# Filling the unused rows of each expert's region during the last batch's attention

## The reference

```python
x = x + tanh(g_xattn) * (self_attention(ln(x)) + cross_attention(ln(x), ctx)) @ Wp + bp   # 16 heads of 16, 1601 context tokens
xf = ln(x).reshape(8192, 256)
scores = softmax(xf @ Wg)                       # 32 experts
weights, indices = top_k(scores, 4)
for e in range(32):
    pos = nonzero(pair_expert == e, size=4096)  # the tokens that chose e
    out = swiglu(xf[tok], W1[e], W2[e], W3[e]) * w[:, None]
    y = y.at[tok].add(out)
x = x + tanh(g_ffn) * (y + swiglu(xf, Ws1, Ws2, Ws3))
```

## Time and profile before

| | us |
|---|---|
| median of 3 runs | 4883.7 (4883.4 to 4888.8) |
| profiled execution | 4891.1 |
| its span | 4888.3 |
| PE busy | 4346.4 (89%) |
| DVE busy | 3532.4 (72%) |
| ACT busy | 2694.8 (55%) |
| POOL busy | 1646.7 (34%) |

### The profile page before, as it was taken

One profiled execution on the slowest core, in us unless ns is written; L12 is line 12 of the kernel. 1 busy time (PEld: TensorE's weight loads), 2 busy tenths in 40 slices (PEclk: granted clock), 3 DMA queues, 4 the chain that ended last, 5 costly groups with the idle time before them and its releaser, 6 DMA issues. The chain is left out here.

```text
span 4888.3 us, 75159 instructions
## 1 busy us (share of the span) xinstructions
PE 4346.4 (89%) x25317; PEld 1904.0 (39%) x25317; DVE 3532.4 (72%) x7733; ACT 2694.8 (55%) x5523; POOL 1646.7 (34%) x2163
## 2 busy tenths in 40 slices
PE   5999999999999999999999999999999995588882
PEld 2333333333343434333333333333333332477771
DVE  5788788787878787878787877887877783244443
ACT  1665656565655556565656565656565653344441
POOL 1122323232323232323232222323232314388883
PEclk7999999999999999999999999999999997799996
DMA  5453545444444444544444444444444443888888
GB/s 115 71 91 73 111 79 104 81 109 78 106 79 100 79 102 77 109 82 109 82 105 85 98 87 97 83 98 90 97 94 97 93 96 118 178 151 150 149 150 244
DMA packets 363500, 513.22 MB, mean 105 GB/s; under 512 B 64124, under 2 KB 227820, under 8 KB 363176
## 3 DMA queue, kind: packets, MB, share of 16 engines
q1 hardware_dynamic: 272592, 385.16, 37.8%
q0 software_dynamic: 87728, 115.39, 13.3%
q10 hardware_dynamic: 2856, 8.52, 0.5%
HBM read 288.49 MB, written 201.27 MB: 100 GB/s over the span
## 5 line engine op out<-in xcount | busy, mean ns | idle before, releaser
L662 ACT ACTIVATE prob<-scores 128x512 f32<-128x512 f32 (+3 forms) x4352 | 2150.3, 561 | 1331.3 <-PE scores L467 1297.4
L849 DVE TENSOR_REDUCE pmx<-ring 128x1 f32<-128x512 f32 (+1 forms) x3328 | 1998.5, 661 | 188.9 <-PE ring L545 175.6
L467 PE MATMUL scores<-stacks 98*128 98x512 bf16 (+3 forms) x4352 | 1272.3, 369 | 70.5 <-ACT prob L662 41.1
L489 PE MATMUL outs<-prob,vt 128*32 128x512 f32 x8704 | 1096.7, 576 | 12.7 <-POOL prob L1051 11.7
L545 PE MATMUL ring<-stacks 96*128 96x512 bf16 x3072 | 984.4, 389 | 90.1 <-DVE pmx L849 80.7
L467 PEld LDWEIGHTS scores<-stacks 98*128 98x128 bf16 (+1 forms) x4352 | 338.5, 99 | 1244.3 <-ACT prob L662 718.7
L849 DVE TENSOR_REDUCE mc<-ring 128x1 f32<-128x128 f32 (+3 forms) x1024 | 437.1, 480 | 147.1 <-PE ring L562 112.1
L1573 POOL DMA_INDIRECT scratch_sums<-e_yo,e_tok x320 | 495.9, 1550 | 118.8 <-issue 86.2
L1051 POOL TENSOR_SCALAR_AFFINE_SELECT prob<-prob 128x512 f32<-128x512 f32 x256 | 167.9, 656 | 1077.0 <-ACT prob L662 1075.2
L545 PEld LDWEIGHTS ring<-stacks 96*128 96x128 bf16 x3072 | 303.2, 99 | 511.4 <-DVE pmx L849 243.8
L1121 POOL TENSOR_TENSOR split<-rest,split 128x512 bf16<-128x512 f32 (+1 forms) x224 | 218.5, 975 | 824.4 <-DVE split L943 823.9
(11 more groups left out here) (165 smaller groups left out, 3752.7 us busy)
## 6 DMA issues: line engine op xcount, KB each, us to landing
stacks<-scratch_parts SPq DMA_DIRECT2D x768, 128.0 KB, 7.1
stacks<-scratch_parts SPq DMA_DIRECT2D x384, 136.1 KB, 10.1
scratch_parts<-split SPq DMA_DIRECT2D x64, 768.0 KB, 4.5
e_xin<-scratch_slots SPq DMA_DIRECT2D x160, 289.0 KB
scratch_parts<-split SPq DMA_DIRECT2D x32, 816.8 KB, 4.4
num<-oc POOLq DMA_DIRECT2D x256, 64.0 KB
den<-scratch_inverses POOLq DMA_DIRECT2D x63, 256.0 KB, 8.9
ct<-in_ctx_t_dram SPq DMA_DIRECT2D x16, 800.5 KB, 8.2
```

The costliest lines, as they stand in the source:

```text
L467: eng.matmul(ps[0:m, k, q0:T], kst[g][0:KR + 2, j, k0:k0 + m], qst[g][0:KR + 2, j, qc + q0:qc + T], start=True, stop=True).then_inc(scored ...
L489: mm = eng.matmul(po[32 * j:32 * j + 32, q0:T], vt[ch][0:m, VW * vi + VE * hl:VW * vi + VE * hl + 32], prob[0:m, n % 2, j, q0:T], start=kt ...
L662: eng.activation(prob[0:m, n % 2, j, q0:T], ps[0:m, i % SB, q0:T], ACT.Exp, scale=SCALE).then_inc(exped.sem, 1)
L849: eng.tensor_reduce(dst, src, AX.X, ALU.max).then_inc(free_of(part, it), 1)
```

## The change

Four things change together.

- The fills move. They are no longer items of part X but of part L: `blank` (POOL) at place 68 + 6, `ends` (DVE) at 68 + 26, and four `fill` items (SP, 8 experts each) at 68 + 30, 40, 50 and 60. The item `rank` of part L is at 68 + 22, so the count known there is that of 15 batches.
- They grow. The last batch may add up to 512 rows to an expert, so each fill writes 768 rows (512 + 256) from the count of 15 batches on, and the last batch's scatter then writes over the first of them. The regions grow with them: `stride` = 4096 + 768. The number of DMAs stays 33 (32 of 768 rows, one of 256).
- The access pattern is another: partition p writes rows 2p and 2p + 1 of each 256, which are one run of 2312 bytes, where it wrote rows p and p + 128 in two runs of 1156 bytes.
- `blank`, `firstz`, a second `ncap` and `zrow` lie in the tile `rest`, which part L doesn't use, and no longer in `prob`. The last batch's scatter on POOL waits until all fills have landed.

```diff
-    stride = cap + GR
+    stride = cap + 3 * GR
...
     if kind == "X":
         f = FINISH
-        return [[x] for x in f[:2] + [("spread",), ("experts", 3)] + f[2:10] + ROUTE + [("table",), ("fill", 0)] + f[10:]
-                + [("fill", 1)] + SCATTER]
+        return [[x] for x in f[:2] + [("spread",), ("experts", 3)] + f[2:10] + ROUTE + [("table",)] + f[10:] + SCATTER]
...
     if kind == "L":
         deal(0, (36, 70, 104), [("experts", i) for i in range(3)], 0.0)
+        deal(HALF, (6, 26, 30, 40, 50, 60), [("blank",), ("ends",)] + [("fill", i) for i in range(4)], 0.0)
...
+        free = rest[:, :, :].rearrange("p a n -> p (a n)")
+        ends = np.cumsum([0, 2 * ROW, E, E, E]).tolist()
+        blank, firstz, ncap_l, zrow = (free[:, a:b] for a, b in zip(ends[:-1], ends[1:]))
...
+                elif what == "ends":
+                    dve.wait_ge(blanked, part, 1)
+                    read(dve, part, ("rank",))
+                    eng.tensor_scalar(ncap_l, cnt[:, :], float(cap), None, ALU.min).then_inc(behind.sem, 1)
+                    dve.wait_ge(behind, part, 1)
+                    eng.tensor_tensor(zrow, ncap_l, firstz, ALU.add).then_inc(behind.sem, 1)
...
                 elif what == "scatter":
                     q, k = it[1:]
+                    if part.kind == "X":
+                        pool.wait_ge(filled, part, 0)
...
                 elif what == "fill":
-                    half = it[1]
-                    sp.wait_ge(tabled, part, 2)
-                    sp.wait_ge(blanked, part, 4)
-                    for e in range(E // 2 * half, E // 2 * (half + 1)):
-                        if e % 8 == 0:
-                            _, ends_at = nc.values_load_multi_w_load_instructions(
-                                zrow[0:1, e:e + 8], engines=[mybir.EngineType.SP], min_val=0, max_val=dump - 1)
-                        fill(scr["slots"][bass.ds(ends_at[e % 8], 256), :])
-                    if half:
-                        fill(scr["slots"][spare_rows:spare_rows + 256, :])
+                    i = it[1]
+                    sp.wait_ge(behind, part, 2)
+                    sp.wait_ge(blanked, part, 3)
+                    _, ends_at = nc.values_load_multi_w_load_instructions(
+                        zrow[0:1, 8 * i:8 * i + 8], engines=[mybir.EngineType.SP], min_val=0, max_val=dump - 1)
+                    for e in range(8):
+                        fill(scr["slots"][bass.ds(ends_at[e], 3 * 256), :], 3)
+                    if i == 3:
+                        fill(scr["slots"][spare_rows:spare_rows + 256, :], 1)
...
-            def fill(rows):
-                eng.dma_start(rows.rearrange("(q p) c -> p q c", p=128), blank[:, :, :]).then_inc(filled.sem, 16)
+            def fill(rows, n):
+                eng.dma_start(rows.rearrange("(n p q) c -> p n (q c)", p=128, q=2),
+                              free[:, 0:2 * ROW].unsqueeze(1).broadcast_to([128, n, 2 * ROW])).then_inc(filled.sem, 16)
```

More of the change, by code:

```diff
@@ L321, in build_attention @@
         late = prob[:, :, :, :].rearrange("p a h n -> p (a h n)")
-        ends = np.cumsum([0, 2 * T, 2 * T, 2 * ROW, E, E, E, E, E, E, NC2, NC2, NC2 * E, NC2 * E, 2 * NC2, 2 * NC2, 128]).tolist()
-        act_x, sig_x, blank, ncap, firstz, gend, gtmp, gint, zrow, gid, gcl, le, les, tab, tmp, tabt = (
+        ends = np.cumsum([0, 2 * T, 2 * T, E, E, E, E, NC2, NC2, NC2 * E, NC2 * E, 2 * NC2, 2 * NC2, 128]).tolist()
+        act_x, sig_x, ncap, gend, gtmp, gint, gid, gcl, le, les, tab, tmp, tabt = (
             late[:, a:b] for a, b in zip(ends[:-1], ends[1:]))
         act_x, sig_x = (s.rearrange("p (m n) -> p m n", m=2) for s in (act_x, sig_x))
-        blank = blank.rearrange("p (q c) -> p q c", c=ROW)
-        gint, zrow, tabt = (s.bitcast(I32) for s in (gint, zrow, tabt))
+        gint, tabt = (s.bitcast(I32) for s in (gint, tabt))
         le, les = (s.rearrange("p (c e) -> p c e", e=E) for s in (le, les))
         tab, tmp = (s.rearrange("p (k c) -> p k c", c=NC2) for s in (tab, tmp))
+        free = rest[:, :, :].rearrange("p a n -> p (a n)")
+        ends = np.cumsum([0, 2 * ROW, E, E, E]).tolist()
+        blank, firstz, ncap_l, zrow = (free[:, a:b] for a, b in zip(ends[:-1], ends[1:]))
+        blank = blank.rearrange("p (q c) -> p q c", c=ROW)
+        zrow = zrow.bitcast(I32)
         gates_of = lambda part: (act_x, sig_x) if part.kind == "X" else (act_t, sig_t)
@@ L371, in build_attention @@
         oned = event("oned", 16, P=8)
-        tabled = event("tabled", X=29)
+        tabled = event("tabled", X=28)
+        behind = event("behind", L=2)
         consts = event("consts", P=CONSTS)
         masked = event("masked", **each(16))
-        blanked = event("blanked", X=4)
+        blanked = event("blanked", L=3, X=1)
         low = event("low", P=14, F=14, M=14)
@@ L403, in build_attention @@
         walled = event("walled", 16, L=30, X=10)
-        filled = event("filled", 16, X=E + 1)
+        filled = event("filled", 16, L=E + 1)
         tab_in = event("tab_in", 16, X=2 * NC2)
@@ L609, in item @@
                     dst = take(part, it)
-                    pe.wait_ge(tabled, part, 29)
+                    pe.wait_ge(tabled, part, 28)
                     eng.transpose(dst[0:2 * NC2, 0:128], tab.rearrange("p k c -> p (k c)"), ident[:, :]).then_inc(ring.sem, 1)
@@ L799, in tables @@
                 per = lambda v: v.unsqueeze(1).broadcast_to([128, NC2, E])
-                dve.wait_ge(blanked, part, 4)
+                dve.wait_ge(blanked, part, 1)
                 read(dve, part, ("rank",))
                 then(eng.tensor_scalar(ncap, cnt[:, :], float(cap), None, ALU.min))
-                then(eng.tensor_tensor(zrow, ncap, firstz, ALU.add))
                 then(eng.tensor_scalar(gint, ncap, 255.0, None, ALU.add))
@@ L1104, in item @@
                         eng.tensor_tensor(xr[:, q, :], xr[:, q, :], bpt[:, :], ALU.add).then_inc(biased.sem, 1)
+                elif what == "blank":
+                    pool.wait_ge(low, part, 0)
+                    eng.iota(firstz, pattern=[[stride, E]], base=0, channel_multiplier=0,
+                             allow_small_or_imprecise_dtypes=True).then_inc(blanked.sem, 1)
+                    eng.memset(blank[:, :, 0:C], 0.0).then_inc(blanked.sem, 1)
+                    eng.iota(blank[:, :, C:], pattern=[[128, 2], [0, 1 + E]], base=tokens, channel_multiplier=1,
+                             allow_small_or_imprecise_dtypes=True).then_inc(blanked.sem, 1)
                 elif what == "scatter":
                     q, k = it[1:]
+                    if part.kind == "X":
+                        pool.wait_ge(filled, part, 0)
                     pool.wait_ge(routed, part, 40)
@@ L1194, in pool_program @@
                      allow_small_or_imprecise_dtypes=True).then_inc(blanked.sem, 1)
[L1195 to L1200, removed]
             run(left)
@@ L1359, in sp_program @@
             for ev, n in ((x1_out, 1), (xn_out, 1), (zeroed, 1), (scattered, 16), (walled, 10),
-                          (filled, E + 1), (tab_in, 2 * NC2)):
+                          (filled, 0), (tab_in, 2 * NC2)):
                 sp.wait_ge(ev, left, n)
```

## The result

The changed kernel takes 4895.8 us (median of 20 runs, 4887.7 to 4906.1), the kernel before 4887.1 in the runs beside it: a ratio of 1.0022 (95% interval 1.0015 to 1.0029), some 9 to 11 us slower. The forecast was 4921, some 38 us slower, with a range of 4882 to 4944. The sign and the place are right; the size is about a quarter of what was said.

A forecast was written before the change was run, and what follows sets the result against it. Compute paces attention; exposed fills hold the block's end. T = 4048.7 + 102.5 + 19 + 3 + 3.7 = 4176.9, less 4138.7 gives +38.2 us on a median of 4883.7: 4922, forecast 4921, range 4882 to 4944.

The forecast's parts named there:

- The chain and the place: Fills on SP's queue delay the last batch's load of x; GpSimd, VectorE and the whole tail wait for it.
- T: Time the load of x lands behind 28.7 MB of fills, forecast 4176.9; net change T - 4138.7, or +38.2 us.
- The gain of 40.1: At the block's end, without exposed fills, the next block starts at 4163.0 instead of 4203.1: 40.1 us gained.
- The start: First fill on SP's queue after row copies and first number load: between 4045.0 and 4052.3, taken as 4048.7.
- The fills' rate: Rate of the moved fills on the DMA engines: 280 GB/s, so 28.7 MB take 102.5 us.
- what stands beside the fills: Traffic and waits around the fills: weights and GpSimd's DMAs 19 us, number loads 3, the load of x 3.7.
- Rival 1: Larger pieces fill at full pace, 412 GB/s; T about 4137, net -2 us, total 4882; chance 0.12.
- Rival 2: A limit per byte written: fills stay at 247 GB/s; T 4201, net +62 us, total 4946; chance 0.14.
- Rival 3: Load of x overtakes the fills; the scatter waits for them instead, net -2 to nearly -40 us; chance 0.06.
- What hides beside attention: From 4045 to attention's end at 4084.7, 40 us of DMA time lie beside attention, at little cost to it.
- Experts' block put at nothing: Experts' stage with regions of 4864 rows for 4352: no added time, as SP waits there for buffers, not bandwidth.

The follow-up runs named there:

- e3: The changed kernel with fills of 1280 rows instead of 768 and regions that much wider; ratio 1.0133 to the kernel before.
- e4: The changed kernel with the load of x for the last residual issued on SP's queue ahead of the fills; ratio 0.9986 to the kernel before.
- e10: The kernel before run again, unchanged, on a third chip; ratio 1.0008, last copy to experts 110.2 us.
- e11: The changed kernel run again on the same chip as e10; ratio 1.0034 to the kernel before, last copy to experts 127.0 us.
- e1: The changed kernel with pieces of 1156 B, three DMAs of 256 rows for each expert; ratio 1.0094 to the kernel before.
- e2: The kernel before with its 33 tail fills of 256 rows in pieces of 2312 B, nothing moved; ratio 0.9994 to the kernel before.
- e5: The changed kernel with each 768-row fill as two DMAs of 384 pieces of 1156 B; ratio 1.0077 to the kernel before.
- e6: The changed kernel with each 768-row fill as three DMAs of 128 pieces of 2312 B; ratio 1.0058 to the kernel before.
- e7: The kernel of e4 with the last part's store and fetch of normalised rows issued on ScalarE's queue; ratio 0.9962 to the kernel before.
- e8: The kernel of e7 with the third group of expert weights behind the fills instead of between them; ratio 0.9947 to the kernel before.

## Why the prediction was right and wrong

- **The chain and the place: right, shown.** The fills queue ahead of the load of x, GpSimd and VectorE wait for it, and the net change is T less a fixed number. T was 4148.4, so T - 4138.7 gives +9.7; measured are +8.4 in the stretch. That these two lie so close is in part luck: the tail slipped by 1.0 us more than the formula says, and the gain was 2.3 more. e3 and e4 show the dependence from both sides.
- **The gain of 40.1: nearly right.** 42.4 measured in that execution, 2.3 more. The block now ends with GpSimd's scatter, 27.6 us from its first issue, and not with the last store: in e4 that store is issued at 4164.2, long before, and the block still ends 27.7 us after the scatter's first issue. But some 8 us of the gain were a slow number load of one profile. Between e10 and e11 the gain is 35.1.
- **The start: 5.2 us too late.** I took the middle between a quick and a slow first number load; it was quick in both profiles of the changed kernel. The scatter beside it alone doesn't make it slow, as I had hinted: e10 has the same scatter and a quick load.
- **The fills' rate: the step that failed.** I took 280 GB/s, by scaling the larger piece's 343 with the fall that the 1156-byte stream shows. The large DMAs of large pieces don't fall: 383 in the changed kernel and for 60 us on end in e3. At 383 the 28.7 MB take 75 us and not 102.5, 27.5 less. From the first fill to T I had said 128.2 us, and 105.0 were measured, 23.2 less, so what stands beside the fills (weights, GpSimd's DMAs, number loads, the load itself) took some 30 us for the 25.7 I had put. I had scaled a property of small DMAs and short pieces, which e1, e2, e5 and e6 show it to be, to a stream that has neither. The 343 has the ramp of a short transfer in it: from 3863.0 to 3865.0, past its ramp, that short store of the kernel before ran at 374 GB/s. Nearly the whole rate was in the trace of the kernel before; what wasn't there is that it lasts.
- **Rival 1** had the rate almost right (412 for 383) and was given 0.12; 380 or more was my own sign for it. Its T of about 4137 is 11 us too early, that of the forecast 28.5 too late. Rival 2 (247 for any piece) is excluded by the 383. Rival 3 doesn't occur: the load landed behind all fills.
- **What hides beside attention: right.** The last copy came at 4083.9 for 4084.7, and GpSimd still idled 13.9 us before its mask.
- **Experts' block put at nothing:** 2.6 and 2.9 us more in the two profiles of the changed kernel, 2.4 in e3, but e1, e5, e7 and e8 with the same wide regions have none. Not settled.

## What to carry to other kernels

A bulk write that nobody waits for still costs as much as everything issued behind it on its queue is late; look for the first small load behind it, and send that earlier or on another engine's queue. A rate taken from a stream holds for its piece length and its DMA size only. Price a new shape from both ends, and weigh the end that shares its shape, here the short store of nearly the same piece, more than the one that shares its purpose. Read the rate of a short transfer from its middle. A second profile of the kernel before, on another chip, would have shown 8 us of the baseline to be unsteady.

## What was not expected of the hardware

- The same bytes to the same rows took 105 us in 33 DMAs of 2312-byte pieces and 143 us in 97 DMAs of 1156-byte pieces; both the piece (26.7 us at 97 DMAs) and the number of DMAs (11.3 us at 2312 B) count.
- The rate of a stream of 296 KB DMAs falls after 3 to 4 us, with pieces of 1156 B (323 to 247) and of 2312 B (389 to 320); with 888 KB DMAs of 2312-byte pieces it stays at 383 for the 25 us of the changed kernel's window, and with 1.5 MB DMAs for the 60 us of e3's.
- The register instructions behind a number load of SP ran at 0.15 us each in most places and at up to 0.7 us in the first group of two executions, the kernel before and e2 (13.3 and 13.2 us from the table's loads to the first fill, for 4.7 in e10). The cause is open.
- A DMA issued behind a full queue landed 11 to 13 us after its issue, whatever the rate: the load of x took 12.5 us in the changed kernel, whose fills run at 383 GB/s, and 11.6 in e1, whose fills run at 251. By the windows of these 12.5 and 11.6 us (331 and 224 GB/s) the engines moved 4.1 and 2.6 MB in them, so the queue holds no fixed number of bytes.
